# Cosine attention: normalised tokens split on their own rows and turned by transposing DMAs

## The reference, cut to what matters

```
v = layernorm(x) @ Wv.T + bv          # 512 x 256
t = ctx @ Wt.T + bt                   # 512 x 256
x = x + (v @ t.T) / max(|v_i| |t_j|, 1e-8)
```

## Time and profile before

| | us |
|---|---|
| median of three runs | 1724.04 |
| lowest, highest run | 1719.91, 1727.51 |
| span of the profiled execution | 1727.3 |
| PE busy in it | 1589.8 |
| DVE busy | 1226.5 |
| ACT busy | 1150.9 |
| POOL busy | 1022.9 |

### The profile page before, as it was taken

One profiled execution on the slowest core, in us unless ns is written; L12 is line 12 of the kernel. 1 busy time (PEld: TensorE's weight loads), 2 busy tenths in 40 slices (PEclk: granted clock), 3 DMA queues, 4 the chain that ended last, 5 costly groups with the idle time before them and its releaser, 6 DMA issues. The chain is left out here.

```text
span 1727.3 us, 29488 instructions
## 1 busy us (share of the span) xinstructions
PE 1589.8 (92%) x8932; PEld 719.8 (42%) x8932; DVE 1226.5 (71%) x1756; ACT 1150.9 (67%) x1895; POOL 1022.9 (59%) x738
## 2 busy tenths in 40 slices
PE   5999878998999977899999999999999978999998
PEld 3545433443444432334444444444443423444443
DVE  4978898997888745676776767676767665665553
ACT  5667599787888744665757666666657567556662
POOL 4776436765678723565657666665756665455452
PEclk9989999999999997999999999999999989999999
DMA  8421000000000122121211212121211200010001
GB/s 309 146 73 32 1 1 1 1 1 1 0 1 1 45 59 81 32 58 25 58 34 36 56 27 57 27 55 32 58 25 40 55 22 28 25 49 24 24 24 49
DMA packets 60463, 72.22 MB, mean 42 GB/s; under 512 B 14416, under 2 KB 40016, under 8 KB 59856
## 3 DMA queue, kind: packets, MB, share of 16 engines
q1 hardware_dynamic: 56944, 62.22, 12.3%
q10 hardware_dynamic: 3424, 8.91, 1.3%
HBM read 37.40 MB, written 8.39 MB: 27 GB/s over the span
## 5 line engine op out<-in xcount | busy, mean ns | idle before, releaser
L1556 DVE TENSOR_REDUCE s_mx<-bank 128x1 f32<-128x512 f32 x512 | 337.3, 685 | 199.8 <-PE bank L1684 193.7
L1443 ACT ACTIVATE s_E<-bank 128x512 f32<-128x512 f32 x512 | 293.9, 595 | 202.5 <-PE bank L1698 177.2
L1342 POOL TENSOR_TENSOR s_E<-s_E 128x1024 f32<-128x1024 f32 x128 | 300.5, 2367 | 125.4 <-PE bank L1706 117.9
L1684 PE MATMUL bank<-s_KA,s_QA 96*128 96x512 f16 x512 | 194.2, 390 | 17.7 <-DMA s_KA<-sm_cx 7.1
L1698 PE MATMUL bank<-s_QA,s_KA 97*128 97x512 f16 x512 | 196.7, 386 | 3.8 <-DMA s_QA<-s_mrow 1.4
L1335 POOL TENSOR_TENSOR sm_cx<-s_qkf,sm_cx 128x512 f16<-128x512 f32 x64 | 76.5, 1195 | 175.6 <-ACT sm_cx L1421 175.4
L1867 POOL TENSOR_TENSOR sm_cx<-m_xf,sm_cx 128x512 f16<-128x512 f32 x60 | 84.1, 1408 | 104.9 <-ACT sm_cx L1909 104.9
L1706 PE MATMUL bank<-s_E,s_V 128*32 128x512 f32 x1024 | 135.6, 602 | 4.3 <-ACT s_E L1443 4.3
L1075 PE MATMUL bank<-sm_zz,w1raw 128*128 128x512 f16 x256 | 100.3, 392 | 31.1 <-DVE sm_cx L962 16.3
L1098 PE MATMUL bank<-f_w2q,w2raw 128*128 128x512 f16 x512 | 122.2, 380 | 0.4 <-ACT w2raw L912 0.4
L772 POOL TENSOR_TENSOR sm_wkv<-sm_wkv,sm_cx 128x511 f32<-128x511 f32 x48 | 66.1, 1378 | 94.2 <-DVE sm_wkv L962 94.1
(11 more groups left out here) (264 smaller groups left out, 4092.1 us busy)
## 6 DMA issues: line engine op xcount, KB each, us to landing
sm_cx<-in_ctx SPq DMA_DIRECT2D x16, 768.0 KB, 4.6
s_QA<-sm_cx SPq DMA_DIRECT2D x384, 32.0 KB, 1.9
s_KA<-sm_cx SPq DMA_DIRECT2D x372, 32.0 KB, 1.9
X<-in_x SPq DMA_DIRECT2D x8, 1024.0 KB, 6.8
out_x<-X SPq DMA_DIRECT2D x8, 1024.0 KB, 4.3
w1raw<-in_w ACTq DMA_DIRECT2D x1, 4096.0 KB, 14.2
w2raw<-in_w ACTq DMA_DIRECT2D x1, 4096.0 KB, 28.7
w1raw<-in_wq SPq DMA_DIRECT2D x1, 1024.0 KB, 5.1
```

Source lines behind the costliest of these rows:

```text
L1342: e.tensor_tensor(into, into, other, ALU.add).then_inc(s_sum.sem, 1)
L1443: e.activation(E[:, SLOT[k] + h, :], SC[u % 2][:, :], ACT.Exp, scale=1.0 / float(np.sqrt(DH)))\
L1556: e.tensor_reduce(mx[:, q, h:h + 1], MX[q % 2][:, :], AX.X, ALU.max).then_inc(s_red.sem, 1)
L1684: e.matmul(MX[k % 2][:, :], QA[0:MROW, m, h, q * P:(q + 1) * P], KA[0:MROW, m, h, :], start=True, stop=True).then_inc(s_mx.sem, 1)
```

## The change

The transposes of PE and both banks' worth of fp32 in PSUM go. ACT writes the high half of a normalised tile with tokens on partitions into `lead`, DVE writes the low half into `rest` (both unused parts of existing buffers), and SP issues for each of the four tiles two transposing DMAs, 128 x 512 fp16 each, which write the turned tile into the columns of `zh` and `zl` that belong to its tokens. PE's token projection waits for `s_turned`, the semaphore that all these DMAs raise. The same is done once more for the first batch of the next stage. The four dot products go to `banks[6:8] + banks[0:2]` in place of `banks[6:8] + banks[2:4]`, so that they share no bank with the projections; `project` keeps its waits on `s_y`. SP's loop over the batches is written out, and the loads of a batch's context stand behind the transposing DMAs.

```
-        T, PB, NT, NV, DB = banks[0:2] + banks[6:8], banks[2:4], banks[4], banks[5], banks[6:8] + banks[2:4]
+        PB, NT, NV, DB = banks[2:4], banks[4], banks[5], banks[6:8] + banks[0:2]
+        lead, rest = env["wkv"][:, 2 * TT * D:3 * TT * D].rearrange("p (q d) -> p q d", d=D), env["rows_of"](env["cx"], 12, 16)
+        s_turned, TURNED = sem("turned"), 2 * TT * 16
...
         @block.sync
+            def turned(b):
+                s_proj.wait(e, b, 0)
+                for q in range(TT):
+                    cols = slice(q * P, (q + 1) * P)
+                    s_zh.wait(e, b, q + 1)
+                    e.dma_start_transpose(zh[:, :, cols], lead[:, q, :]).then_inc(s_turned, 16)
+                    s_zl.wait(e, b, q + 1)
+                    e.dma_start_transpose(zl[:, :, cols], rest[:, q, :]).then_inc(s_turned, 16)
+            tokens(1)
+            turned(0)
+            context(1)
+            for b in range(1, B):
+                if b + 1 < B:
+                    tokens(b + 1)
+                turned(b)
+                if b + 1 < B:
+                    context(b + 1)
+            turned(B)
+            e.wait_ge(s_turned, (B + 1) * TURNED)
...
         @block.scalar
-            def high(b, c):
-                s_proj.wait(e, b, 0)
-                s_T.wait(e, b, c + 1)
-                e.activation(zh[:, c, :], T[c][:, :], ACT.Copy).then_inc(s_zh.sem, 1)
+            def high(b, q):
+                if b and q == 0:
+                    e.wait_ge(s_turned, b * TURNED)
+                if b < B:
+                    s_z.wait(e, b, q + 1)
+                else:
+                    s_r2.wait(e, 0, q + 1)
+                e.activation(lead[:, q, :], z[:, q, :], ACT.Copy).then_inc(s_zh.sem, 1)
...
         @block.vector
-            def low(b, c):
-                s_zh.wait(e, b, c + 1)
-                e.tensor_tensor(zl[:, c, :], T[c][:, :], zh[:, c, :], ALU.subtract).then_inc(s_zl.sem, 1)
+            def low(b, q):
+                s_zh.wait(e, b, q + 1)
+                if b and q == 0:
+                    e.wait_ge(s_turned, b * TURNED)
+                e.tensor_tensor(rest[:, q, :], z[:, q, :], lead[:, q, :], ALU.subtract).then_inc(s_zl.sem, 1)
...
         @block.tensor
                 if i == KH:
-                    s_zl.wait(e, b, KD)
+                    e.wait_ge(s_turned, (b + 1) * TURNED)
...
-                for c in range(KD):
-                    transposed(b + 1, c, b)
```

More of the change, by code:

```diff
@@ L248, in steps @@
                 step(b, b == B - 1)
-        credit(nc, [*credited, *env["f_credited"]])
+        credit(nc, [*credited, *env["f_credited"]], [f_T])
         block = ctx.enter_context(nc.Block())
@@ L262, in _, with tokens, context @@
             e.dma_start(cb[:, :], cb_d).then_inc(s_bias, 16)
-            def body(b):
+            def tokens(b):
                 s_x.wait(e, b, 0)
-                e.dma_start(X[:, bass.ds(b * (TT * D), TT * D)].rearrange("p (q d) -> p q d", d=D),
-                            x_d[bass.ds(b * S, S), :].rearrange("(q p) d -> p q d", p=P)).then_inc(s_x.sem, 16)
+                e.dma_start(X[:, b * (TT * D):(b + 1) * (TT * D)].rearrange("p (q d) -> p q d", d=D),
+                            x_d[b * S:(b + 1) * S, :].rearrange("(q p) d -> p q d", p=P)).then_inc(s_x.sem, 16)
+            def context(b):
                 s_cl.wait(e, b, 0)
-                e.dma_start(cf[:, :, :], ctx_d[bass.ds(b * DC, DC), :].rearrange("(c p) s -> p c s", p=P))\
+                e.dma_start(cf[:, :, :], ctx_d[b * DC:(b + 1) * DC, :].rearrange("(c p) s -> p c s", p=P))\
                     .then_inc(s_cf.sem, 16)
-            batches(e, 1, B, body)
+            def turned(b):
[17 more added lines that the diff above has]
+            e.wait_ge(s_turned, (B + 1) * TURNED)
         @block.gpsimd
@@ L347, in normalised @@
                 s_nmr.wait(e, b, 2)
-                s_T.wait(e, b, 0)
+                s_zl.wait(e, b, 0)
                 e.activation(z[:, q, :], tile(b, q), ACT.Identity, bias=nmr[:, q:q + 1], scale=rstd[:, q:q + 1])\
@@ L370, in _ @@
             wa(e, (1,))
-            for c in range(KD):
-                high(0, c)
+            for q in range(TT):
+                high(0, q)
             e.wait_ge(s_bias, 64)
@@ L383, in settled @@
                 e.activation(w1q[:, piece], raw[0][:, piece], ACT.Identity, bias=nround[:, 0:1])
[L385 to L388, removed]
             e.wait_ge(s_const, 6)
@@ L411, in step @@
                         settled(QUANT[b])
[L412 to L416, removed]
+                for q in range(TT):
+                    high(b + 1, q)
             steps(e, step)
@@ L505, in _ @@
             wvec(e)
-            for c in range(KD):
-                low(0, c)
+            for q in range(TT):
+                low(0, q)
             def step(b, last):
@@ L512, in step @@
                 else:
-                    s_T.wait(e, b, KD)
+                    s_zl.wait(e, B, 0)
                     f_normalise(e, 0)
@@ L534, in step @@
                 weigh(b, 3)
[L535 to L539, removed]
+                for q in range(TT):
+                    low(b + 1, q)
                 if b == STATS_AT:
@@ L606, in total @@
                 e.matmul(NV[:, 8 + i:9 + i], ones[:, :], totals[:, i:i + 1], start=True, stop=True).then_inc(s_wp, 1)
[L608 to L621, removed]
             e.wait_ge(s_lo, 1)
```

5 lines of the change are left out of this document (1 added, 4 removed).

## The result

The changed kernel takes 1811.56 us (median of four runs, 1809.26 to 1813.79) where the kernel before, beside it, takes 1724.97 (1719.91 to 1727.51): 1.0507 times as long, 95% interval 1.0482 to 1.0533, 86.6 us more. The forecast was 1835, and slower.

The account below looks back on a forecast made before the run. TensorE (PE) was taken as the bound; eight later waits 94.9, batch 0 9.2 and clock 6.9 made 111 us on 1727.3, so 1838, or 1835 as median. Range 1791 to 1867 (chance 0.47); eight in ten 1750 to 1950.

Parts of the forecast that it names:

- Nothing gained on PE: Context projection still waits for the previous batch's third weighted tile, so removing 1.75 us of transposes gains 0.3 us per even step.
- Seven DMAs behind low half 0: On SP, seven of a set's eight transposing DMAs issue after the first low half; PE idles some 12 us before token projection.
- D: Time one 128x512 transposing DMA takes of SP's queue: 1.9 us taken, from packets; forecast range 1.2 to 2.4.
- rival (1): Transposing DMAs as cheap as copies, D = 0.6: 2.8 us late, 1746 to 1766; chance 0.25 including what lies up to the forecast.
- The tail of 1.3 us: After a transposing DMA's time on SP's queue, 1.3 us remain until its semaphore, which the token projection awaits.
- Batch 0: First set lands at 34.7 against the token projection's 25.53: 9.2 us late; weight loads sharing the engines can only add.
- The clock: PE's lower clock after each wait costs 8 x 2.5 = 20 us, less 13.1 already in three slow steps: net 6.9.
- the three slow steps of before: First-stage steps of 24.2 to 24.7 us, already at the lower clock; their 13.1 us taken as moved, not doubled.
- The low halves: DVE's low halves, reading SBUF in place of PSUM: 683 ns each taken, 870 the other end, 0.7 us a set, hidden.
- The rest of SP's queue: Context and token loads issued behind the eight transposing DMAs, near 77 us; ACT wants the context later, so free.
- Rival (3): Transposed halves ready before token projection wants them: 6.8 us gained in steps, 3.3 at the start, at best 1714; chance 0.04.

## Why the prediction was right, and where its sizes were off

**Nothing gained on PE: right.** The first context matmul starts at 93.37, 0.14 us after the third weighted tile (92.55 + 0.68), released by it. Taking that wait away gains nothing either (1811.32): behind it stands the wait for the DMAs.

**Seven DMAs behind low half 0: right in form.** Issued in a close train, the first at 95.15 behind the first low half; a wait between context and token projection in every batch.

**D, the time of one, mis-sized: 1.31 us, not 1.9.** The forecast took the mean packet of SP's queue, 0.060 us, for each of 512 pieces. The count is borne out (39168 packets more, 36864 of them would be 72 DMAs of 512). But they are cheap: the queue's share went from 12.3% of 16 x 1727.3 to 14.3% of 16 x 1806.4, 734 us more, 0.019 us a packet, so 512 on 16 engines are 0.6 us. What decides is the instruction on SP, 1.27 us for half of it or the whole, as the split set showed. The bound at which the forecast had put rival (1), D = 0.6, was the copy's hold on SP; the transposing instruction holds it twice as long. With D = 1.31 the forecast's own formula gives 63.98 + 9.2 + 1.3 = 74.5, 7.8 us late against 66.72, and eight such are 62; the trace has 56.9 in seven and 10.6 at the end, 67.5, in place of 94.9. The tail of 1.3 us was right (2.5 from issue to landing, 1.27 of them on SP). The Trainium skill, "DMA: Bandwidth & Descriptors", section "Latency and other measured facts", has 261 GB/s, by which 128 KB are an estimated 0.5 us; that is near those 0.6 us of the engines and says nothing of SP. The Trainium skill, "VectorE: DVE Perf Modes", section "The three transpose paths", has 1309 ns for one 128x128 block by DMA. Here an instruction of four such blocks held SP for 1265 ns and one of two for 1245; a single block was not run.

So the range was met in part by luck. It ran from D = 1.2 to 2.4, and 1.31 lies in it, but neither packets nor blocks set D. With the true D and its other terms as they stand the forecast would have said 62 + 5.1 + 6.9 = 74 us more, 1798, and the error of the next term closes the gap.

**Batch 0, mis-sized: 19.0 us, not 9.2.** The forecast said that the weight loads "can only add" and then added nothing. They add 14: one DMA of the train held SP for 6.31 us, and with the loads held back it is 1.26. This error has the other sign and hid a third of the first.

**The clock: about right.** 20 less 13.1 was forecast; the twin with PE kept busy shows 15.2, less the same 13.1, 2.1. In the steps' 58.6 us all that is not waiting for the DMAs (56.9) nets to 1.7: this has the clock in it, the transposes that are gone (12.3) and the longer waits for the weighted tile (9.9). That the three slow steps of before would be moved and not doubled was right: all steps are now 30 to 31 us.

**The low halves: beyond the other end.** 1035 ns in the mean, not 683 or 870, and 1.5 us more for the four of the step shown (3.97 against 2.47 us). Only the first of them is on the path: the train is slower than they are. The median is 686 (forecast 683); single ones take up to 1757.

**The rest of SP's queue: right.** PE, ACT and DVE show no wait for a context or token load beyond the first one, which was there before (6.4 and 8.6 us).

**The sum.** Forecast 94.9 + 9.2 + 6.9 = 111; measured 67.5 + 19.0 + 1.7 = 88.2 in the first stage (the 1.7 with all that the paragraph on the clock lists), and 86.6 between the medians.

**Rival (3).** It was said to need the low halves ahead of the weighted tiles. Moving them there takes three more reorderings on ACT, POOL and the statistics. Then the steps give 9.3 us where the rival had 6.8, most of it in the slow steps, and DVE's chain, which the rival itself named, seems to bound the later ones. What it did not see are the ends: no 3.3 us are won at the start (1.6 are lost), and the last stretch costs 7.8. What comes out is a tie.

## What to carry to other kernels

A transposing DMA between SBUF buffers is priced by the instruction, about 1.3 us of the issuing queue and 2.5 us to landing for 128x256 and 128x512 fp16 alike; count the instructions between the last producer and the first reader, before the bytes. Work that an engine did in sequence with its reader (PE's transposes, 1.75 us) may not be given to a queue behind the same producer unless the producer moves ahead by the train's length. And before an engine is relieved, look at which engine is next: here DVE was within 1.3 us of PE in an even step and the change gave it 11 us more in the stage, so the best version measured ties.

## What was not expected of the hardware

- The hold on SP: 1245 ns for 128x256, 1265 for 128x512, 1857 for 128x2048 (medians); landing 2.4, 2.5 and 4.6 us. The large one moves 512 KB at some 280 GB/s by its hold, the small one 64 KB at 53.
- Beside bulk loads of 4 MB such a DMA held SP for up to 6.3 us and landed up to 16.5 us after its issue. Four in a row took 12.3 us where they take 5.1 alone.
- The low half with all operands in SBUF takes 0.65 to 0.69 us with POOL idle, up to 1.76 in the changed kernel and up to 2.8 with the halves moved ahead. Where the rows stand beside each other in time, the slow ones fall beside POOL's work on SBUF: two took 3.36 us beside POOL's context low half. From PSUM all were 0.68 to 0.69. That POOL is the cause was not tried by itself. The rows are DVE's and POOL's timelines of the kernel with the halves moved ahead:

```profile
129.91 3.36 DVE L454 TENSOR_TENSOR sm_cx<-sm_wkv 128x512 f16<-128x512 f32 x2
```

```profile
129.03 3.09 POOL L313 TENSOR_TENSOR sm_cx<-sm_cx 128x1536 f16<-128x1536 f32 x1 [1.74 <-ACT sm_cx L386]
```
